# A down product copied from PSUM in one piece, its halves summed later from SBUF, and seven table values loaded per round on TensorE

## The chip, the core and the metric

The kernel runs on one core of a Trainium2 chip. The core has five engines with instruction queues of their own: TensorE (PE in the rows, its weight loads PEld), VectorE (DVE), ScalarE (ACT), GpSimd (POOL) and SyncE (SP), which here only issues transfers. They meet through semaphores. The metric is the device time of one launch in microseconds. Three runs of the kernel before took 306.15, 307.87 and 311.05 us.

## The reference

Two sequences of 1024 tokens of width 256 go through a layer norm and a cross attention to 77 context rows, then a layer norm and a feed-forward part with one shared expert and 32 routed ones, of which each token takes one:

```python
x = x + xattn(layernorm(x), ctx, ctx, mask, ...)
h = layernorm(x).reshape(-1, 256)
shared = (silu(h @ shared_gate) * (h @ shared_up)) @ shared_down     # 256 -> 512 -> 256
logits = h @ gate_w                                                  # 32 experts
e = argmax(logits); score = sigmoid(max(logits))
g, u = (h * score) @ routed_gate[e], (h * score) @ routed_up[e]      # 256 -> 512
routed = (silu(g) * u) @ routed_down[e]                              # 512 -> 256
x = x + shared + routed
```

All of it is in float32. An expert has 1.5 MB of weights: 0.5 MB each for gate, up and down.

## The kernel before, in words

Attention, norms and routing come first. The tokens are then sorted by expert with indirect transfers, and the shared expert's products fill TensorE in between. What matters here is the **expert loop** behind that.

The sorted tokens are cut into *chunks* of 32 tokens of one expert, at least one chunk for each expert: 79 with these inputs, in experts of 3, 3, 2, 2, 5, 1, 7, 2, 5, 1, 1, 3, ... chunks. A table in SBUF (chunk_cum, made on VectorE) holds where each expert's chunks end, counted from the first. TensorE's loop is a hardware loop over 5 *rounds* of 6 experts, and a rest of 2 experts. The weights lie in a ring of 6 slots (ring_gu, ring_d): SyncE refills a slot (refill, L355) with the expert 6 further on as soon as the last chunk of the expert in it has its gate and up products (u_done), then the down weights (down_done). SyncE takes the slots strictly in order.

A chunk goes through the engines thus:

- GpSimd copies the chunk's 32 columns of the transposed tokens to x_c, in two halves (L455, L457). For this it loads the chunk's first column from a table each time (L453).
- TensorE does the gate and up products (gate_up, L1016) into bank 0 and bank 1 of PSUM, 16 matmuls each that count as 32 passes in the profile. It may overwrite bank 0 when Silu has read it (silu_done) and bank 1 when the gated product has read it (h_ready).
- ScalarE does Silu of bank 0 (L775), VectorE multiplies by bank 1 (gated, L643) and transposes (turn_h, L647) into the single buffer hT, when the down product of the chunk before has read it (down_done).
- TensorE does the down product (down_of, L1038) into bank 2. The two halves of the inner sum lie on partitions 0 to 63 and 64 to 127, and have to be added.
- ScalarE copies the low half to SBUF (take_half, L780), VectorE adds the high half to it from PSUM (take_y, L653) and signals y_ready. The next down product waits for y_ready, since there is one bank for it.
- Every 16 chunks ScalarE issues two stores of finished rows (store_y, L783).

TensorE's order is skewed by one chunk: the gate and up products of a chunk stand ahead of the down product of the chunk before. Written out, expert() does an expert's first chunk (L1047 to L1054), in whose middle the sequencer loads turn_end, where the expert ends. The remaining chunks follow in an inner loop behind a branch (L1056 to L1059). At a round's start it also loads turn_first (L1064). Each value_load is a TENSOR_LOAD and two instructions that check the value's range (shown as ISA in lists of instructions, as FUSED_REGOPS and SEQ_ASSERT in the trace).

Behind the loop the last stores land, GpSimd gathers the rows back in token order (L462, 16 transfers), VectorE adds them to the residual and SyncE writes them out.

## Time and profile before

| | |
|---|---|
| Runs, us | 306.15, 307.87, 311.05; median 307.87 |
| The profiled execution, us | 305.98 |
| its span, first to last instruction, us | 304.2 |
| mean granted TensorE clock | 0.974 |
| TensorE matmuls busy | 261.5 us, 86% |
| VectorE, ScalarE, GpSimd busy | 51%, 31%, 29% |
| Moved by DMA | 68.69 MB, mean 226 GB/s |
| Gate, up and down products of the expert loop, busy | 86.5 us and 51.0 us |

Busy time is a share of the whole span. The span has stages with different limits, so the table does not say what a change in the expert loop is worth. That is read from the timeline of the loop, where each line gives the start, the length, the engine, the line of the kernel, what is written and read, and in brackets how long the engine had been idle and which instruction ended that. "issue" means that nothing the profile shows was waited for.

### The profile page before, as it was taken

The numbers are of one execution on the slowest core, as the hardware profiler recorded it, in microseconds if no ns is written. First come the engines' busy times: TensorE is split into PE (matmuls) and PEld (weight loads), VectorE is DVE, ScalarE is ACT, GpSimd is POOL, SyncE is SP. The second block draws the span as 40 slices with busy tenths as digits, with TensorE's granted clock in tenths as the row PEclk, the third lists the DMA queues.
The fourth block names the chain that finished last, engine by engine and source line by source line (L and its number), as shares of the span: only waits on it lengthen the run. The fifth ranks groups of instructions, "written<-read, shape, count | busy, mean of one in ns | idle before, by whom it ended". The sixth has DMA issues, their size and how long they took to land.

```text
span 304.2 us, 12929 instructions
## 1 busy us (share of the span) xinstructions
PE 261.5 (86%) x4628; PEld 183.6 (60%) x4629; DVE 155.4 (51%) x490; ACT 93.7 (31%) x284; POOL 88.0 (29%) x248
## 2 busy tenths in 40 slices
PE   4978999998798999979889999899899899889710
PEld 3736656653473488657667777677677677643600
DVE  0547877884599321145454555455455455423423
ACT  2056766542311102243232333233233233212000
POOL 1245121111017764022222222222222222202772
PEclk9996899999999999999999999999999999999995
DMA  6999994000002235209989599999999999524575
GB/s 197 343 371 374 375 372 147 0 3 2 0 0 95 103 99 188 69 4 321 321 291 312 155 317 301 367 386 385 371 375 382 384 371 373 186 48 110 165 207 163
DMA packets 53039, 68.69 MB, mean 226 GB/s; under 512 B 3966, under 2 KB 35099, under 8 KB 53019
## 3 DMA queue, kind: packets, MB, share of 16 engines
q1 hardware_dynamic: 46203, 61.60, 58.9%
q0 software_dynamic: 1536, 4.20, 4.5%
q10 hardware_dynamic: 5280, 2.62, 3.3%
q8 instruction: 13, 0.21, 0.3%
q14 instruction: 7, 0.06, 0.1%
HBM read 59.49 MB, written 8.91 MB: 225 GB/s over the span
## 4 chain that ended last, share of the span: by engine, by line
PE 70%; DVE 8%; issue 7%; POOL 5%; DMA 4%; ACT 4%; POOLq 1%; ACTq 1%; SPq 1%; DVEq 0%
PE bank L1016 26%; PE bank L1038 15%; PE bank L941 13%; PE bank L953 5%; POOL xs_flat L462 4%; PE bank L872 3%; PE bank L907 2%; DMA slot_rows<-late 2%; DVE h_place L530 1%; PE bank L890 1%; DVE h_place L531 1%; DMA bq_row<-in_L_xattn_bias_q_dram 1%; ACT h_place L740 1%; DMA xs_flat<-slot_rows,slot_i 1%; PE bank L845 1%
## 5 line engine op out<-in xcount | busy, mean ns | idle before, releaser
L1016 PE MATMUL bank<-ring_gu,x_c 128*32 128x128 f32 x2528 | 86.5, 275 | 7.9 <-issue 5.9
L1016 PEld LDWEIGHTS bank<-ring_gu,x_c 128*32 128x32 f32 x2528 | 65.9, 109 | 23.3 <-issue 20.5
L1038 PE MATMUL bank<-ring_d,h_place 128*32 128x128 f32 x1264 | 51.0, 276 | 4.4 <-DVE late L653 1.0
L455 POOL COPY x_c<-xs_flat 128x32 f32 x79 | 16.6, 210 | 99.1 <-PE bank L1016 86.6
L1038 PEld LDWEIGHTS bank<-ring_d,h_place 128*32 128x32 f32 x1264 | 32.2, 108 | 19.3 <-issue 17.1
L643 DVE TENSOR_TENSOR h_place<-h_place,bank 128x128 f32<-128x128 f32 x79 | 22.7, 288 | 40.2 <-ACT h_place L775 40.2
L780 ACT COPY late<-bank 64x128 f32 (+1 forms) x79 | 20.5, 259 | 51.9 <-PE bank L1038 51.9
L775 ACT ACTIVATE h_place<-bank 128x128 f32<-128x128 f32 x79 | 21.9, 278 | 44.0 <-PE bank L1016 44.0
L647 DVE STREAM_TRANSPOSE h_place<-h_place 128x128 f32<-128x128 f32 x79 | 24.6, 311 | 14.4 <-PE bank L1038 9.8
L953 PE MATMUL bank<-shd,h_place 128*128 128x256 f32 x128 | 28.4, 380 | 2.1 <-DVE h_place L531 2.1
L653 DVE TENSOR_TENSOR late<-bank,late 64x128 f32 x79 | 23.1, 293 | 13.8 <-ACT late L780 12.5
L953 PEld LDWEIGHTS bank<-shd,h_place 128*128 128x128 f32 x128 | 24.2, 190 | 6.7 <-DVE h_place L531 3.0
L530 DVE SCALAR_TENSOR_TENSOR h_place<-h_place,bank 128x512 f32<-128x512 f32 x16 | 11.0, 686 | 32.4 <-ACT h_place L740 32.4
L941 PE MATMUL bank<-late,shg 128*128 128x512 f32 x48 | 23.1, 603 | 4.4 <-DVE h_place L531 4.3
L740 ACT ACTIVATE h_place<-bank 128x512 f32<-128x512 f32 x16 | 9.6, 597 | 52.0 <-PE bank L941 52.0
L941 PE MATMUL bank<-late,shu 128*128 128x512 f32 x48 | 22.6, 592 | 0.0
L457 POOL COPY x_c<-xs_flat 128x32 f32 x79 | 16.6, 210 | 17.1 <-PE bank L1016 16.9
L462 POOL DMA_INDIRECT xs_flat<-slot_rows,slot_i x16 | 15.2, 951 | 17.0 <-DMA slot_rows<-late 12.4
L438 POOL DMA_INDIRECT sorted_rows<-xs_flat,pos x16 | 16.1, 1006 | 11.1 <-DVE pos L593 6.5
L941 PEld LDWEIGHTS bank<-late,shg 128*128 128x128 f32 x48 | 8.5, 190 | 13.0 <-issue 7.2
L941 PEld LDWEIGHTS bank<-late,shu 128*128 128x128 f32 x48 | 9.1, 190 | 11.5 <-issue 11.5
L872 PE MATMUL bank<-ident,xs_flat 128*128 128x128 f32 x64 | 10.8, 295 | 2.0 <-DVE xs_flat L514 0.7
(133 smaller groups left out, 255.7 us busy)
## 6 DMA issues: line engine op xcount, KB each, us to landing
ring_gu<-L_ffn_routed_gate_w_dram SPq DMA_DIRECT2D x32, 512.0 KB, 8.5
ring_gu<-n_L_ffn_routed_up_w_dram SPq DMA_DIRECT2D x32, 512.0 KB, 9.5
ring_d<-L_ffn_routed_down_w_dram SPq DMA_DIRECT2D x32, 512.0 KB, 9.9
slot_rows<-late ACTq DMA_DIRECT2D x10, 256.0 KB, 5.8
x<-in_x_dram SPq DMA_DIRECT2D x4, 512.0 KB, 6.8
slot_rows<-zeros SPq DMA_DIRECT2D x1, 2048.0 KB, 14.4
late<-sorted_rows SPq DMA_DIRECT2D x8, 256.0 KB, 3.3
out_dram<-x SPq DMA_DIRECT2D x8, 256.0 KB, 2.4
```

The source lines that it names most:

```text
L455: g_.tensor_copy(x_c[:, 0], xsT[:, 0, bass.ds(col, LW)]).then_inc(x0_part, 1)
L462: g_.indirect_dma_start(out=y_t[:, i, :], out_offset=None, in_=slot_rows, in_offset=bass.IndirectOffsetOnAxis(ap=slot_i[:, i:i + 1], axis= ...
L643: v.tensor_tensor(h_r, g_silu, bank[1][:, 0:P], ALU.mult).then_inc(h_ready, 1)
L647: v.transpose(hT, h_r).then_inc(hT_ready, 1)
L653: v.tensor_tensor(rows, bank[2][HR:P, 0:DH], rows, ALU.add).then_inc(y_ready, 1)
L775: a_.activation(g_silu, bank[0][:, 0:P], ACT.Silu).then_inc(silu_done, 1)
L780: a_.copy(y_all[:, bass.ds(c, 1)].rearrange("p c d -> p (c d)"), bank[2][0:HR, 0:DH]).then_inc(half_taken, 1)
L872: ins = te.transpose(dst[:, c:c + P], src[:, a + j, k * P:(k + 1) * P], ident[:])
L941: ins = te.matmul(dst[:], w[:, k, m * P:(m + 1) * P], xnT_of(g)[:, k], start=(k == 0), stop=(k == KD - 1))
L953: ins = te.matmul(bank[4 + w % 2][:, j * D:(j + 1) * D], h_s[:, w // 2 % 2, m, c:c + P], shd[:, m], start=(m == 0), stop=(m == KF - 1))
L1016: ins = te.matmul(bank[g][q * LW:(q + 1) * LW, 0:P].rearrange("p (m f) -> p m f", f=LW), x_c[:, k], columns[:, q], start=(k == 0), stop=(k ...
L1038: ins = te.matmul(bank[2][r:r + LW, 0:DH], hT[:, f * LW:(f + 1) * LW], ring_d[:, s, f, a * DH:(a + 1) * DH], start=(m == 0), stop=(m == HA ...
```

## The change

Four things change together.

1. take_y moves to ScalarE and copies the whole 128 partitions of the down product to SBUF in one instruction. It signals a new semaphore, y_taken, and the next down product waits for this instead of y_ready.
2. The sum of the two halves (sum_y) is done by VectorE with both operands in SBUF, one chunk later than before: in the loop behind the transpose of chunk c it sums chunk c-2. Two sums follow the loop. y_ready now counts sums alone, so the stores' waits lose their offset of 2.
3. The tables turn_first and turn_end become one table, turn, with 1 in front. At the start of a round TensorE loads seven neighbouring values of it at once (three for the rest), and none inside the round.
4. The round is rotated. The first gate and up products are done ahead of the loop; in a round each expert first does its remaining chunks (other_chunks), then the first gate and up products of the next expert followed by its own last down product (next_expert). The branch on the first round goes. The products come in the same order as before.

```diff
-        y_all = late[0:HR, 0:SLOTS * DH].rearrange("p (c d) -> p c d", c=SLOTS)
+        y_halves = late[:, 0:SLOTS * DH].rearrange("p (c d) -> p c d", c=SLOTS)
+        y_all = y_halves[0:HR]
...
-            v.tensor_scalar(turn_end[:], chunk_cum[0:1], 1.0, None, ALU.add).then_inc(table_ready, 1)
-            v.scalar_tensor_tensor(out=turn_first[:], in0=chunk_cum[0:1], scalar=1.0, in1=chunk_f[0:1],
-                                   op0=ALU.add, op1=ALU.subtract).then_inc(table_ready, 1)
+            v.memset(turn[:, 0:1], 1).then_inc(table_ready, 1)
+            v.tensor_scalar(turn[:, 1:NE + 1], chunk_cum[0:1], 1.0, None, ALU.add).then_inc(table_ready, 1)
...
-            def take_y(c):
-                dve.wait_ge(half_taken, c + 1)
-                rows = y_all[:, bass.ds(c, 1)].rearrange("p c d -> p (c d)")
-                v.tensor_tensor(rows, bank[2][HR:P, 0:DH], rows, ALU.add).then_inc(y_ready, 1)
+            def sum_y(c):
+                dve.wait_ge(y_taken, c + 1 + FREE2)
+                sums = y_all[:, bass.ds(c, 1)].rearrange("p c d -> p (c d)")
+                other = y_halves[HR:P, bass.ds(c, 1)].rearrange("p c d -> p (c d)")
+                v.tensor_tensor(sums, other, sums, ALU.add).then_inc(y_ready, 1)
...
-            with dve.Fori(1, n_chunks) as c:
+            gated(1)
+            dve.wait_ge(down_done, 1)
+            turn_h(1)
+            with dve.Fori(2, n_chunks) as c:
                 gated(c)
                 dve.wait_ge(down_done, c)
                 turn_h(c)
-                take_y(c - 1)
-            take_y(n_chunks - 1)
+                sum_y(c - 2)
+            sum_y(n_chunks - 2)
+            sum_y(n_chunks - 1)
...
-            def take_half(c):
+            def take_y(c):
                 act.wait_ge(down_done, c + 1)
-                a_.copy(y_all[:, bass.ds(c, 1)].rearrange("p c d -> p (c d)"), bank[2][0:HR, 0:DH]).then_inc(half_taken, 1)
+                a_.copy(y_halves[:, bass.ds(c, 1)].rearrange("p c d -> p (c d)"), bank[2][:, 0:DH]).then_inc(y_taken, 1)
...
-                        act.wait_ge(y_ready, STORE * b + FREE2)
+                        act.wait_ge(y_ready, STORE * b)
...
             def down_of(w, s):
                 pe.wait_ge(hT_ready, w)
-                pe.wait_ge(y_ready, w)
+                pe.wait_ge(y_taken, w)
...
-            def expert(w, e, s, before, landed):
-                pe.wait_ge(gu_in[s], 2 * landed)
-                gate_up(w, s)
-                end = pe.value_load(turn_end[0:1, bass.ds(e, 1)], min_val=2, max_val=MAX_CHUNKS + 1)
-                if before is None:
-                    with pe.If(it > 0):
-                        down_of(w, RING - 1)
-                else:
-                    down_of(w, before)
+            def turns(e, n):
+                _, values = nc.values_load_multi_w_load_instructions(
+                    turn[0:1, bass.ds(e, n)], engines=(mybir.EngineType.PE,), min_val=1, max_val=MAX_CHUNKS + 1)
+                return values
+            def other_chunks(w, end, s, landed):
                 pe.wait_ge(d_in[s], landed)
                 with pe.If(w + 1 < end):
                     with pe.Fori(w + 1, end) as more:
                         gate_up(more, s)
                         down_of(more, s)
                     pe.nop()
-                return end
+            def next_expert(end, s, landed):
+                n = (s + 1) % RING
+                pe.wait_ge(gu_in[n], 2 * landed)
+                gate_up(end, n)
+                down_of(end, s)
+            pe.wait_ge(gu_in[0], 32)
+            gate_up(1, 0)
             with pe.Fori(0, ROUNDS) as it:
-                w = pe.value_load(turn_first[0:1, bass.ds(RING * it, 1)], min_val=1, max_val=MAX_CHUNKS)
+                w = turns(RING * it, RING + 1)
                 for s in range(RING):
-                    w = expert(w, RING * it + s, s, s - 1 if s else None, 16 * it + 16)
+                    other_chunks(w[s], w[s + 1], s, 16 * it + 16)
+                    next_expert(w[s + 1], s, 16 * it + (16 if s + 1 < RING else 32))
...
```

The first place is the start of a round on TensorE's queue. Before, with the load of turn_first ahead of the gate and up products (L1016) and that of turn_end behind them, ahead of the down product (L1038):

```order
L1063 UNCONDITIONAL_BRANCH
L1063 ISA
L1064 TENSOR_LOAD turn_first
L1064 ISA x2
L1047 ISA
L1016 MATMUL bank<-ring_gu,x_c 32x128 [waits silu_done,x0_part,gu_in0]
...
L1016 MATMUL bank<-ring_gu,x_c 32x128 x7
L1049 REGISTER_ALU
L1049 TENSOR_LOAD turn_end
L1049 ISA x2
L1051 COMPARE_AND_BRANCH
L1038 MATMUL bank<-ring_d,h_place 32x128 [waits y_ready,hT_ready]
```

Now the same place, and what follows it up to the inner loop (gate and up products are L1020, down products L1042):

```order
L1020 MATMUL bank<-ring_gu,x_c 32x128 x7
L1072 UNCONDITIONAL_BRANCH
L1072 ISA
L1050 TENSOR_LOAD turn
L1050 ISA x14
L1056 ISA
L1057 REGISTER_ALU [waits d_in0]
L1057 COMPARE_AND_BRANCH
L1058 UNCONDITIONAL_BRANCH
L1020 MATMUL bank<-ring_gu,x_c 32x128 [waits silu_done,x0_part]
```

The seven loads of a round have become one, at its start, with fourteen instructions of checks behind it, and the checks of all seven values stand ahead of the first product that follows; between gate and down products nothing is left.

The second place is VectorE's loop over chunks. Before:

```order
L642 REGISTER_ALU [waits u_done,silu_done]
L643 TENSOR_TENSOR h_place<-h_place,bank 128x128 [waits hT_ready]
L647 STREAM_TRANSPOSE h_place<-h_place 128x128 [waits h_ready,down_done]
L653 ISA [waits half_taken]
L653 TENSOR_TENSOR late<-bank,late 64x128
```

Now:

```order
L641 REGISTER_ALU [waits u_done,silu_done]
L642 TENSOR_TENSOR h_place<-h_place,bank 128x128 [waits hT_ready]
L646 STREAM_TRANSPOSE h_place<-h_place 128x128 [waits h_ready,down_done]
L653 ISA [waits y_taken]
L653 REGISTER_ALU
L653 TENSOR_TENSOR late<-late 64x128
```

The sum stands where the add stood, but it is that of the chunk before, and its input from PSUM (bank) is gone.

## Rows read from the trace of the kernel before

**Rows 1.** The page: clock granted, DMA engines' share, GB/s, in 40 slices.

```profile
PEclk9996899999999999999999999999999999999995
DMA  6999994000002235209989599999999999524575
GB/s 197 343 371 374 375 372 147 0 3 2 0 0 95 103 99 188 69 4 321 321 291 312 155 317 301 367 386 385 371 375 382 384 371 373 186 48 110 165 207 163
```

**Rows 2.** Timeline, inner loop: start us, us, engine line op tiles count [idle before <-releaser].

```profile
164.32 0.65 PE L1038 MATMUL bank<-ring_d,h_place 128*32 128x128 f32 x16
...
165.04 0.31 DVE L647 STREAM_TRANSPOSE h_place<-h_place 128x128 f32<-128x128 f32 x1
165.11 0.26 ACT L780 COPY late<-bank 64x128 f32 x1 [0.58 <-PE bank L1038]
165.52 0.29 DVE L653 TENSOR_TENSOR late<-bank,late 64x128 f32 x1 [0.17 <-ACT late L780]
...
165.96 0.64 PE L1038 MATMUL bank<-ring_d,h_place 128*32 128x128 f32 x16
```

**Rows 3.** Timeline where TensorE comes sooner than its inputs.

```profile
171.26 0.21 POOL L457 COPY x_c<-xs_flat 128x32 f32 x1
...
171.32 1.18 PE L1016 MATMUL bank<-ring_gu,x_c 128*32 128x128 f32 x32
171.64 0.59 PEld L1016 LDWEIGHTS bank<-ring_gu,x_c 128*32 128x32 f32 x24 [0.16 <-DVE h_place L643]
...
172.32 0.21 POOL L455 COPY x_c<-xs_flat 128x32 f32 x1 [0.85 <-PE bank L1016]
172.35 0.28 ACT L775 ACTIVATE h_place<-bank 128x128 f32<-128x128 f32 x1 [0.44 <-PE bank L1016]
...
172.61 0.64 PE L1038 MATMUL bank<-ring_d,h_place 128*32 128x128 f32 x16
...
172.75 0.29 DVE L643 TENSOR_TENSOR h_place<-h_place,bank 128x128 f32<-128x128 f32 x1 [0.39 <-ACT h_place L775]
```

**Rows 4.** Timeline of TensorE: first product of rounds four and six.

```profile
216.72 1.08 PE L1016 MATMUL bank<-ring_gu,x_c 128*32 128x128 f32 x32 [1.02 <-issue]
...
262.03 1.08 PE L1016 MATMUL bank<-ring_gu,x_c 128*32 128x128 f32 x32 [0.82 <-issue]
```

**Rows 5.** Sequencer instructions between two rounds: ns min/median/max, first, last start us.

```profile
L1064 PEldq TENSOR_LOAD <-turn_first x1: 309/309/309, 241.7 to 241.7; - x1
L1064 PEldq FUSED_REGOPS  x1: 146/146/146, 242.1 to 242.1; - x1
...
L1047 PEldq FUSED_REGOPS  x1: 51/51/51, 242.4 to 242.4; - x1
```

**Rows 6.** Timeline of TensorE: chunk products that the sums count from.

```profile
132.93 1.09 PE L1016 MATMUL bank<-ring_gu,x_c 128*32 128x128 f32 x32 [1.60 <-ACT h_place L775]
133.84 0.62 PE L1038 MATMUL bank<-ring_d,h_place 128*32 128x128 f32 x16
...
148.66 0.85 PE L1016 MATMUL bank<-ring_gu,x_c 128*32 128x128 f32 x20 [0.67 <-issue]
...
181.44 1.08 PE L1016 MATMUL bank<-ring_gu,x_c 128*32 128x128 f32 x32
...
266.94 1.08 PE L1016 MATMUL bank<-ring_gu,x_c 128*32 128x128 f32 x32
...
269.74 0.65 PE L1038 MATMUL bank<-ring_d,h_place 128*32 128x128 f32 x16 [1.01 <-DVE late L653]
```

**Rows 7.** Weight transfers: two issues in the timeline, and us to landing.

```profile
182.73 0.38 SPq L311 DMA_DIRECT2D ring_gu<-L_ffn_routed_gate_w_dram  x1
...
253.80 1.16 SPq L315 DMA_DIRECT2D ring_d<-L_ffn_routed_down_w_dram  x1
...
ring_d<-L_ffn_routed_down_w_dram SPq DMA_DIRECT2D x1, 512.0 KB, 10.2
```

More of the change, by code:

```diff
@@ L188, in build_cross_attention_moe @@
         begin = sb("begin", [1, P], I32)
-        turn_first = sb("turn_first", [1, NE], I32)
-        turn_end = sb("turn_end", [1, NE], I32)
+        turn = sb("turn", [1, NE + 1], I32)
         block_n = sb("block_n", [1, 1], I32)
@@ L269, in build_cross_attention_moe @@
         begin_ready = sem("begin_ready")
-        half_taken = sem("half_taken")
+        y_taken = sem("y_taken")
         g_done = sem("g_done")
@@ L793, in _ @@
                 if j:
-                    take_half(j - 1)
+                    take_y(j - 1)
             with act.Fori(1, blocks) as b:
@@ L797, in _ @@
                     silu(STORE * b + j)
-                    take_half(STORE * b + j - 1)
+                    take_y(STORE * b + j - 1)
                     if j == 3:
-                        act.wait_ge(y_ready, STORE * b + FREE2)
+                        act.wait_ge(y_ready, STORE * b)
                     if j in (3, 8):
@@ L804, in _ @@
                 silu(c)
-                take_half(c - 1)
-            take_half(n_chunks - 1)
-            act.wait_ge(y_ready, STORE * blocks + FREE2)
+                take_y(c - 1)
+            take_y(n_chunks - 1)
+            act.wait_ge(y_ready, STORE * blocks)
             for a in range(HALVES):
                 store_y(blocks - 1, a)
-            act.wait_ge(y_ready, n_chunks + FREE2)
+            act.wait_ge(y_ready, n_chunks)
             for a in range(HALVES):
@@ L819, in _ @@
             te = nc.tensor
-            for credit in (y_ready, y_ready, silu_done, h_ready, hT_ready, x0_used, u_done):
+            for credit in (y_taken, y_taken, silu_done, h_ready, hT_ready, x0_used, u_done):
                 pe.sem_inc(credit, FREE1)
@@ L1060, in expert @@
                     pe.nop()
-                return end
+            def next_expert(end, s, landed):
[5 more added lines that the diff above has]
+            gate_up(1, 0)
             with pe.Fori(0, ROUNDS) as it:
-                w = pe.value_load(turn_first[0:1, bass.ds(RING * it, 1)], min_val=1, max_val=MAX_CHUNKS)
+                w = turns(RING * it, RING + 1)
                 for s in range(RING):
-                    w = expert(w, RING * it + s, s, s - 1 if s else None, 16 * it + 16)
-            w = pe.value_load(turn_first[0:1, RING * ROUNDS:RING * ROUNDS + 1], min_val=1, max_val=MAX_CHUNKS)
+                    other_chunks(w[s], w[s + 1], s, 16 * it + 16)
+                    next_expert(w[s + 1], s, 16 * it + (16 if s + 1 < RING else 32))
+            w = turns(RING * ROUNDS, REST + 1)
             for s in range(REST):
-                w = expert(w, RING * ROUNDS + s, s, s - 1 if s else RING - 1, 16 * ROUNDS + 16)
+                other_chunks(w[s], w[s + 1], s, 16 * ROUNDS + 16)
+                if s + 1 < REST:
+                    next_expert(w[s + 1], s, 16 * ROUNDS + 16)
             down_of(n_chunks + 1, REST - 1)
             shared_up(3 * KF + 1)
-            pe.wait_ge(y_ready, n_chunks + FREE2)
+            pe.wait_ge(y_taken, n_chunks + FREE2)
             shared_up(3 * KF + 2)
```

## The prediction

> **What bounds the kernel now.** I read the slices of the page first [rows 1]. The expert loop fills slices 18 to 36 (130.3 to 270.4 us), with the TensorE clock at full all through it. From slice 26 to 34 the DMA engines are 9 tenths busy at 367 to 386 GB/s, before that they have holes. So two things can set the pace: the loop of engines, and behind it, in its second half, the stream of expert weights.
>
> The timeline of the inner loop [rows 2] then shows which wait ends last. A down product starts at 164.32 and the next at 165.96: 1.64 us for a chunk. Between them ScalarE copies the low half (it starts 0.79 after the product), VectorE adds the high half (0.41 later, since the transpose that starts at 165.04 is ahead of it), the add takes 0.29, and 0.15 after its end the next product starts: 0.79 + 0.41 + 0.29 + 0.15 = 1.64. This cycle through one PSUM bank is closed by y_ready, and it sets the chunk.
>
> The next cycle is seen where TensorE happens to come early [rows 3]. The gate and up products start at 171.32 and stop after 8 weight loads, until the gated product of the chunk before is out of the banks (h_ready); they go on at 171.64. From there: Silu 0.71 later, the gated product 0.40 after that, 0.29 long, and, as at 171.64, some 0.05 to TensorE: 1.45 us. TensorE itself needs less: 0.91 from the gate products to the down product [rows 6], and some 0.4 for the down product, 1.3 in all.
>
> In the same rows the down product starts 1.29 after its gate products (171.32 to 172.61) rather than 0.91. This is the first chunk of an expert, where TensorE's sequencer loads turn_end between the two.
>
> **The change, part by part.**
>
> *One copy, the sum later.* The down product now waits for the copy alone: 0.79 + 0.26 + 0.15 = 1.20, and for the transpose: 0.72 + 0.31 + 0.15 = 1.18 [rows 2]. Both are under 1.45, so the cycle of rows 3 becomes the bound. The copy covers 128 partitions instead of 64; its cost is by the column, as the Silu of 128x128 at 0.28 beside the copy of 64x128 at 0.26 shows [rows 3, 2], so I add 0.02 at most, hidden. The add keeps its size and moves one chunk later; VectorE has 0.29 + 0.31 + 0.29 of work in 1.45, so it is hidden, unless it disturbs another engine (rivals). The last sum before the stores is the same in both kernels.
>
> *The table loads.* Before, 32 loads stand between gate and down products at some 0.3 us of delay each; they go, and with y_ready gone nothing but 1.45 holds these chunks either. The rotated round itself issues the same products in the same order. From the second chunk's gate products (132.93) to the last chunk's (266.94) [rows 6] there are 77 periods in 134.0 us, 1.74 each with everything. After: 77 x 1.45 = 111.7. The stall of 0.67 before 148.66 has no semaphore behind it; I keep it.
>
> *The round's start.* Before, TensorE idles 1.02 us between rounds and 0.82 at the last one [rows 4]: branch, one load, one check. The load takes 0.4 to its check (241.7 to 242.1), the check of one value 0.3 (242.1 to 242.4) [rows 5]. Seven values come in one load instruction but with seven pairs of checks. Nothing shows a seven-word load; I take it as one, and 0.28 for each further check. Between rounds that is 6 x 0.28 = 1.7, plus 0.3 for the wait and the branch of the inner loop that now stand there, less 0.2 that the sequencer has in hand when it no longer waits for y_ready: idle 2.8. The period there is 0.91 + 0.64 + 2.8 = 4.3 instead of 1.45, so 2.85 on top, four times: 11.4. At the last boundary three values: 0.82 + 2 x 0.28 + 0.3 - 0.2 = 1.5 idle, 1.6 + 1.4 - 1.45, about 1.4 on top. The bounds for one further check are its two instructions alone, 0.16, and a whole load with check, 0.7; 0.28 is nearest to the row.
>
> *The first round.* Its seven loads come behind the first gate products. The sequencer is done with those at about 130.5; branch, load, seven checks, wait and inner loop take 3.2, so the second chunk starts at 133.7 rather than 132.93: 0.8 lost.
>
> TensorE alone: 111.7 + 11.4 + 1.4 + 0.7 = 125.2 against 134.0, 8.8 saved, less 0.8: 8.0.
>
> *The stream.* The DMA engines are last not full around 182 to 184; then the gate weights issued at 182.73 start a stretch that is full up to the last down weights, issued at 253.80 and landed 10.2 later, at 264.0 [rows 7, 1]. The last chunk's gate products come at 266.94, 2.9 later. That slack is all there is: the stretch moves the same bytes at the same rate, so it ends earlier only by as much as it begins earlier. It begins when the 30th chunk's products (181.44) free their slot. Up to there are 28 periods, 48.5 us before; after, 28 x 1.45 + 2.85 + 0.7 = 44.2, so 4.3 less 0.8: 3.5 earlier. The last down weights land at 260.5, and with 0.3 of waits and branch the last gate products start at 260.8, 6.1 earlier, where TensorE alone would be 8.0 earlier. TensorE therefore waits some 2 us for weights near the end.
>
> *The end.* From the last gate products to the start of the last down product it takes 2.80 (266.94 to 269.74), after it 0.91 + 1.20 = 2.1: 0.7 more. From there to the end the chain runs through stores, GpSimd's gathers and the output, which the change leaves alone.
>
> **Sum:** 6.1 + 0.7 = 6.8, I take 6.9 with a tenth for the copy's earlier start. Against the profiled execution's 305.98 (span 304.2 and 1.8 around it) that is 299.1. The median of the runs is 307.87, 1.9 above the profiled one; at the same distance I expect 301.0.
>
> **The rivals.**
>
> 1. *The period falls only to 1.52 or more.* GpSimd needs 1.06 from its second copy to the next first one (171.26 to 172.32) [rows 3] and at least 0.2 to the next second: near 1.3. The new sum reads two SBUF operands, once per chunk, just when the copy of x_c is due. If one holds up the other by its 0.29, GpSimd needs 1.5 to 1.6. Then 77 x 0.07 = 5.4 or more of the 8.8 goes: 3.4 saved, 304.5; at 1.56 nearly nothing. For it speaks only the closeness; against it that the delay need not fall on the same path each time. The Trainium skill has this rule in "SBUF — State Buffer", section "SBUF: two separate sides": VectorE with two SBUF inputs and a GpSimd operation that reads SBUF exclude each other for the whole instruction. No row here has that pair side by side, so whether the trace agrees is open. Chance 0.15.
>
> 2. *The stream doesn't move.* If transfers are late for another reason than the slot release at 182.7, the last weights still land at 264.0 and 2.9 - 0.3 + 0.7 = 3.3 is all: 304.6. Chance 0.12.
>
> 3. *The stream gives way.* The part up to slice 25 runs below the later rate; with issues coming sooner it may catch up. Then TensorE alone counts, 8.0 + 0.7: 299.2, or 298 with cheaper checks. Chance 0.12.
>
> 4. *Slower: the clock falls between rounds.* TensorE stands for 2.8 us instead of 1.0, four times. The page shows the clock down in slices 4 and 5 [rows 1], some 7 us at half, and no fall at the gaps of 1.0 and 1.6 in the loop [rows 4, 6]. If each new gap costs 7 us at half clock, a chunk there needs 2 x 1.3 = 2.6, 2.7 chunks lose 1.15 each, 3.1 a time, 12.4 in all: 8.7 - 12.4, so 3.7 slower, 311.6. It decides from three falls on. Chance 0.06. The Trainium skill, "TensorE: Matmul & The Clock Gate", section "What's actually happening", says that activity releases the throttle and idleness brings it back; the rows agree in direction.
>
> 5. *Slower: a seven-word load costs as seven loads.* Six more at 0.4 on four rounds, two at the last, six at the first: 12.8 lost, 4.1 slower, 312.0. The single load instruction speaks against it. Chance 0.05.
>
> **How the numbers follow.** The forecast has 0.5, with 5 to 8 us saved (299.9 to 302.9), since the checks (0.16 to 0.35) move both the rounds and the release of the slot. A difference of 2 per cent, 6.2 us or below 301.7, is about what a measurement of this kernel tells from none. About two thirds of the forecast's case (0.33), rival 3 (0.12) and little else lie below: 0.47 faster. Rivals 1 and 2, the rest of the forecast and most of 4 and 5 (under 314.0) are within: 0.49. Slower by more: 0.04. The range from 297.8 to 306.5 takes in the forecast, rivals 2 and 3 and most of rival 1, and leaves out 4 and 5.
>
> **What would show it.** In the timeline: down products 1.45 apart in the inner loop, with weight loads of the gate products held by the gated product; 0.9 between gate and down products in an expert's first chunk; idle of 2.8 between rounds and 1.5 at the last, clock at full; and waits of TensorE for ring_gu or ring_d only in the last two experts. Periods above 1.5 with TensorE waiting for x_c would mean rival 1. The prediction is wrong above all if the gaps between rounds exceed 4 us, or if the last weights do not land near 260.5.

## The result: slower by 2.9 per cent, where a little faster was forecast

| | before | after |
|---|---|---|
| median of 4 runs each, us | 307.01 (306.07 to 311.05) | 315.46 (313.24 to 317.93) |
| the profiled execution, us | 305.98 | 313.24 |
| its span, us | 304.2 | 311.3 |
| mean granted clock | 0.974 | 0.941 |

The ratio is 1.029, 95% interval 1.018 to 1.040. So it is slower, though the runs do not settle whether by more than 2 per cent. The forecast was 301.0, range 297.8 to 306.5, with 0.04 on slower by more than 2 per cent. Here and below the medians are of all runs, while the ratios are taken to runs of the kernel before made beside them and compare the fast runs alone, since some executions of a kernel are slower without any change to it.

### The profile page after: what moved, and what is told of

It is laid out like the page before. It is cut to its first block, busy times and chain, and to the rows that moved or that the text cites. A ratio compares the mean times of both kernels' runs of the same rounds, so it can differ in the third digit from the quotient of the medians.

```text
span 311.3 us, 12946 instructions
## 1 busy us (share of the span) xinstructions
PE 258.1 (83%) x4627; PEld 192.1 (62%) x4629; DVE 154.6 (50%) x490; ACT 94.1 (30%) x284; POOL 87.8 (28%) x248
## 4 chain that ended last, share of the span: by engine, by line
PE 68%; issue 10%; DVE 8%; POOL 5%; DMA 3%; ACT 3%; POOLq 1%; ACTq 1%; SPq 0%; DVEq 0%
PE bank L1020 27%; PE bank L945 13%; PE bank L1042 12%; PE bank L957 4%; POOL xs_flat L462 4%; PE bank L876 3%; PE bank L911 2%; DMA slot_rows<-late 2%; DVE h_place L530 1%; PE bank L894 1%; DVE h_place L531 1%; ACT h_place L744 1%; DMA xs_flat<-slot_rows,slot_i 1%; DMA h_place<-in_L_xattn_kernel_q_dram 1%; PE bank L849 1%
## 5 line engine op out<-in xcount | busy, mean ns | idle before, releaser
L1020 PE MATMUL bank<-ring_gu,x_c 128*32 128x128 f32 x2528 | 97.3, 287 | 24.1 <-issue 23.7
L1020 PEld LDWEIGHTS bank<-ring_gu,x_c 128*32 128x32 f32 x2528 | 68.6, 114 | 41.9 <-issue 27.6
L1042 PE MATMUL bank<-ring_d,h_place 128*32 128x128 f32 x1264 | 53.0, 284 | 0.6 <-DVE h_place L646 0.6
L1042 PEld LDWEIGHTS bank<-ring_d,h_place 128*32 128x32 f32 x1264 | 39.3, 115 | 0.9 <-DVE h_place L646 0.8
L784 ACT COPY late<-bank 128x128 f32 (+1 forms) x79 | 21.0, 265 | 42.6 <-PE bank L1042 42.6
L957 PE MATMUL bank<-shd,h_place 128*128 128x256 f32 x128 | 30.1, 396 | 2.1 <-DVE h_place L531 2.1
L957 PEld LDWEIGHTS bank<-shd,h_place 128*128 128x128 f32 x128 | 25.3, 199 | 7.2 <-DVE h_place L531 3.0
L653 DVE TENSOR_TENSOR late<-late x79 | 22.4, 284 | 3.3 <-ACT late L784 0.8
```

The source lines that it names most:

```text
L653: v.tensor_tensor(sums, other, sums, ALU.add).then_inc(y_ready, 1)
L784: a_.copy(y_halves[:, bass.ds(c, 1)].rearrange("p c d -> p (c d)"), bank[2][:, 0:DH]).then_inc(y_taken, 1)
L957: ins = te.matmul(bank[4 + w % 2][:, j * D:(j + 1) * D], h_s[:, w // 2 % 2, m, c:c + P], shd[:, m], start=(m == 0), stop=(m == KF - 1))
L1020: ins = te.matmul(bank[g][q * LW:(q + 1) * LW, 0:P].rearrange("p (m f) -> p m f", f=LW), x_c[:, k], columns[:, q], start=(k == 0), stop=(k ...
L1042: ins = te.matmul(bank[2][r:r + LW, 0:DH], hT[:, f * LW:(f + 1) * LW], ring_d[:, s, f, a * DH:(a + 1) * DH], start=(m == 0), stop=(m == HA ...
```

## The profile after

The page of the changed kernel, in the view of [rows 1]:

```profile
PEclk9996999999999999979996999999979989999785
DMA  6999992000002354009978199999999999615564
GB/s 204 350 372 371 371 375 85 0 3 2 0 18 105 110 161 148 0 6 315 347 259 298 34 313 345 371 387 381 372 370 317 377 374 374 230 29 113 168 206 162
```

Slices are 7.8 us long. In the expert loop, slices 18 to 36, the clock dips four times (slices 18, 22, 30 and 33); in [rows 1] it does not.

The inner loop in the timeline, to be laid beside [rows 2, 3]:

```profile
210.62 0.62 PE L1042 MATMUL bank<-ring_d,h_place 128*32 128x128 f32 x16
210.65 0.28 ACT L779 ACTIVATE h_place<-bank 128x128 f32<-128x128 f32 x1 [0.45 <-PE bank L1020]
...
211.05 0.29 DVE L642 TENSOR_TENSOR h_place<-h_place,bank 128x128 f32<-128x128 f32 x1 [0.43 <-ACT h_place L779]
...
211.39 0.27 ACT L784 COPY late<-bank 128x128 f32 x1 [0.46 <-PE bank L1042]
211.39 0.59 PEld L1020 LDWEIGHTS bank<-ring_gu,x_c 128*32 128x32 f32 x24 [0.17 <-DVE h_place L642]
211.44 0.31 DVE L646 STREAM_TRANSPOSE h_place<-h_place 128x128 f32<-128x128 f32 x1
211.78 0.28 DVE L653 TENSOR_TENSOR late<-late  x1
...
212.07 0.62 PE L1042 MATMUL bank<-ring_d,h_place 128*32 128x128 f32 x16
212.09 0.21 POOL L455 COPY x_c<-xs_flat 128x32 f32 x1 [0.88 <-PE bank L1020]
```

Down products are 1.45 apart (1.64 in [rows 2]). The weight loads of the gate products stop until the gated product is out, as in [rows 3]: the cycle that the prediction named is now the bound. The copy of 128 partitions takes 0.27 (0.26 for 64 before), the sum from SBUF 0.28. The sum ends at 212.06, just ahead of GpSimd's copy, and neither is longer than before. The copy comes 0.70 after the weight loads go on (211.39 to 212.09), as in [rows 3], where no sum of two SBUF operands was near (171.64 to 172.32, 0.68).

The timeline of TensorE at the start of the loop, at a stall in the first round, at the second, third, fourth and fifth round, and at the end:

```profile
134.37 1.94 PE L1020 MATMUL bank<-ring_gu,x_c 128*32 128x128 f32 x32 [3.25 <-issue]
...
153.44 0.38 PE L1020 MATMUL bank<-ring_gu,x_c 128*32 128x128 f32 x2 [2.59 <-issue]
...
162.30 0.62 PE L1042 MATMUL bank<-ring_d,h_place 128*32 128x128 f32 x16
167.08 1.93 PE L1020 MATMUL bank<-ring_gu,x_c 128*32 128x128 f32 x32 [4.16 <-issue]
168.76 1.11 PE L1042 MATMUL bank<-ring_d,h_place 128*32 128x128 f32 x16
169.61 1.96 PE L1020 MATMUL bank<-ring_gu,x_c 128*32 128x128 f32 x32
...
200.90 1.08 PE L1020 MATMUL bank<-ring_gu,x_c 128*32 128x128 f32 x32 [3.50 <-issue]
201.77 0.65 PE L1042 MATMUL bank<-ring_d,h_place 128*32 128x128 f32 x16
202.24 1.18 PE L1020 MATMUL bank<-ring_gu,x_c 128*32 128x128 f32 x32
...
225.56 1.08 PE L1020 MATMUL bank<-ring_gu,x_c 128*32 128x128 f32 x32 [4.10 <-issue]
226.43 1.04 PE L1042 MATMUL bank<-ring_d,h_place 128*32 128x128 f32 x16
227.17 2.01 PE L1020 MATMUL bank<-ring_gu,x_c 128*32 128x128 f32 x32
...
252.85 1.08 PE L1020 MATMUL bank<-ring_gu,x_c 128*32 128x128 f32 x32 [3.46 <-issue]
253.72 1.02 PE L1042 MATMUL bank<-ring_d,h_place 128*32 128x128 f32 x16
254.44 2.01 PE L1020 MATMUL bank<-ring_gu,x_c 128*32 128x128 f32 x32
...
274.72 1.18 PE L1020 MATMUL bank<-ring_gu,x_c 128*32 128x128 f32 x32
...
276.91 0.81 PE L1042 MATMUL bank<-ring_d,h_place 128*32 128x128 f32 x16 [0.57 <-DVE h_place L646]
```

The second to fifth rounds begin behind idle of 4.16, 3.50, 4.10 and 3.46, the last behind 1.67. Before, the second began behind 1.38, the next three behind 1.02 and the last behind 0.82 (two of these in [rows 4]). Behind the gap at 167.08 the gate and up products take 1.93 instead of 1.08, and the next chunk begins 2.53 later, not 1.45: TensorE runs at 1.2 GHz. The table by stage (stretch, its length, busy time and count, granted clock, DMA share, GB/s) shows it as a clock of 0.63 in a stretch behind a gap, beside one between gaps:

```profile
172.00:197.00 25.00, 24.63 (x816) 1.00 0.75 251
225.50:229.60 4.10, 4.04 (x95) 0.63 1.06 371
```

Lastly the sequencer's instructions of the round loads (ns min/median/max, first and last start):

```profile
L1050 PEldq FUSED_REGOPS  x38: 146/146/151, 131.7 to 271.1; - x38
L1050 PEldq SEQ_ASSERT  x38: 18/18/18, 131.9 to 271.3; - x38
L1050 PEldq TENSOR_LOAD <-turn x6: 775/1084/1717, 130.6 to 269.7; - x6
```

The checks are what they were. The load of seven words takes 1.08 or 1.72, against 0.309 for one word in [rows 5]: 1.09, 1.72, 1.08, 1.71 and 1.08 at rounds one to five, and 0.78 for the three words of the last.

## The experiments

**Theory A** from here on: the period is 1.45 as forecast and worth its gain; the loss comes from the round's start alone, where the load is three to six times as long as taken, and where the longer idle lets the clock fall. The rivals differ by experiment.

### Each half of the change alone

The first kernel takes the one copy and the later sum, with the expert loop of before. The second takes the rotated loop and leaves the down product's way as it was.

```diff
 # copy alone: bank 2 out in one copy, the sum a chunk later; loop as before
-  a_.copy(y_all..., bank[2][0:HR, 0:DH]).then_inc(half_taken, 1)
+  a_.copy(y_halves..., bank[2][:, 0:DH]).then_inc(y_taken, 1)
-  pe.wait_ge(y_ready, w)
+  pe.wait_ge(y_taken, w)
 # loads alone: the rotated loop with turns(), y_ready as before
-  w = expert(w, RING * it + s, s, ...)
+  other_chunks(w[s], w[s + 1], s, ...); next_expert(w[s + 1], s, ...)
```

> The whole-height copy on ScalarE with the sum one chunk later, but TensorE's expert loop and its table loads as before. Theory A (the copy is a gain, the loads cost): down products inside an expert 1.45 us apart, an expert's first chunk still 1.8, idle between rounds 1.0 and the clock at full through the loop; 46 chunks gain 0.1 to 0.15 each, so 4 to 6 us faster than before, near 302. Theory B (the sum from two SBUF operands or TensorE's denser work costs): GpSimd's copies of x_c or the clock suffer here too, and it is as slow as the change, near 315.

> The rotated round with its seven loads at once, but the down product copied and added as before. Theory A: idle of 3.4 to 4.2 us between rounds, the clock at half behind most of them, and chunks 1.64 apart: slower than before by 12 to 18 us, near 322, and slower than the whole change. Theory B: no slower than before, 307 or less, since the loads leave the experts' first chunks.

Measured: copy alone 303.40 (ratio 0.986, interval 0.982 to 0.991); loads alone 327.99 (1.067, 1.055 to 1.079). The copy gains and the loads lose, as Theory A says, though the loads cost more than its 12 to 18 us. They cost 20.4 us on top of before and 12.1 on top of the copy, and the periods from gate products to gate products say why. In the third round of the loads-alone kernel the first chunk of each further expert takes 1.76 to 1.82, as in before (1.77 to 1.81), since y_ready holds it anyway: the loads moved there give nothing back. With the copy alone these chunks take 1.84 to 1.99 (a few, behind an expert of one chunk, 1.71 to 1.74), in the change 1.45: some 22 x 0.42 is 9 us, which the gaps then cost and more.

These first chunks are one reason why the copy alone gains 4 us and not the 8.0 that I forecast for TensorE alone. The other is smaller, some 1.2 us, and is in its timeline of TensorE, near the end:

```profile
256.35 1.08 PE L1022 MATMUL bank<-ring_gu,x_c 128*32 128x128 f32 x32 [0.79 <-DMA ring_gu<-n_L_ffn_routed_up_w_dram]
...
260.46 1.08 PE L1022 MATMUL bank<-ring_gu,x_c 128*32 128x128 f32 x32 [0.69 <-DMA ring_gu<-n_L_ffn_routed_up_w_dram]
...
262.33 1.08 PE L1022 MATMUL bank<-ring_gu,x_c 128*32 128x128 f32 x32 [0.21 <-issue]
```

TensorE waits for weights twice there, as forecast for a faster loop. The last down weights land at 261.7, and the last gate products start 0.6 later.

### Fewer checks in the gap, and the clock held up

One kernel loads the seven values as the change does, but checks only two of them ahead of the round and each other one between an expert's gate and down products. The other leaves the checks and puts four products of 512 columns, which nothing reads, ahead of each round's load.

```diff
 # checks spread
-  turn[...], engines=(PE,), min_val=1, max_val=MAX_CHUNKS + 1)
+  turn[...], engines=(PE,), min_val=None, max_val=None)
+  w[0], w[1] = checked(w[0]), checked(w[1])      # ahead of the round
+  w[s + 2] = checked(w[s + 2])                   # behind gate_up of expert s + 1
 # filled gap
   with pe.Fori(0, ROUNDS) as it:
+      for _ in range(4):
+          te.matmul(bank[3][:], shg[:, 0, 0:P], xnT_last[:, 0], start=True, stop=True)
       w = turns(RING * it, RING + 1)
```

> The whole change, but the seven values are loaded without their range checks; two are checked at the round's start, each other one between the gate and down products an expert ahead of its use. Theory A with the checks as the larger part of the idle time: idle between rounds falls by 1.4 us, to 2.1, or 2.7 where the load is a long one, the clock falls less often, and the time comes to 300 to 307. If the load itself is what costs, idle falls by under 0.5 and the time stays over 312.

> The whole change, with four more 128x512 float32 matmuls into an unused bank ahead of the loads of each round of the loop, 3.4 us of array work that nobody reads, in the place of idle time. If the clock's fall behind the gaps is a real part of the loss, the clock stays at full in the loop and it is 5 to 7 us faster than the change, near 309. If the clock is only a sign, the time stays at 315 or rises by what the matmuls stick out of the gap.

Measured: checks spread 304.53 (0.993, 0.988 to 0.998), as expected; filled gap 307.57 (1.001, 0.996 to 1.007), a little faster than expected. The filled gap, in the timeline of TensorE at the second round:

```profile
161.84 3.70 PE L1074 MATMUL bank<-xnT_last,shg 128*128 128x512 f32 x8
166.43 1.08 PE L1020 MATMUL bank<-ring_gu,x_c 128*32 128x128 f32 x32 [0.90 <-issue]
167.30 0.65 PE L1042 MATMUL bank<-ring_d,h_place 128*32 128x128 f32 x16
167.78 1.18 PE L1020 MATMUL bank<-ring_gu,x_c 128*32 128x128 f32 x32
```

TensorE does 3.70 us more work here, the chunk behind the round starts 0.34 later than in the change (6.05 from gate products to gate products, not 5.71), and the kernel is 8 us faster. No stretch of its expert loop is at half clock. That is the clock's part, told apart from the gap's length: the stretches from round to round are no shorter (by the four periods 0.7 longer in all), and most of the loss is gone. In the profiles the loop from second to last chunk is 8.2 shorter (132.15 and 140.35). Of that 6.2 are the half-clock chunks, counted below, which the fillers removed. Another 0.9 is a shorter stall near 150 us and 0.8 one near 147 that is not there; nothing shows that the fillers did that, so I put 6 of the 8 us down to the clock.

With spread checks the gaps are 2.00 to 2.68, and the clock still falls behind three of four, as behind this one:

```profile
193.17 1.91 PE L1020 MATMUL bank<-ring_gu,x_c 128*32 128x128 f32 x32 [2.04 <-issue]
```

### The load by itself

The loads of 1.72 all started at words 6 and 18 of the table, those of 1.08 at words 0, 12 and 24. The next kernel gives each round a row of eight words; another loads all eight of them (four at the last round). Both have spread checks.

```diff
-  turn = sb("turn", [1, NE + 1], I32)
+  turn = sb("turn", [1, 8 * (ROUNDS + 1)], I32)
...
-  w = turns(RING * it, RING + 1)
+  w = turns(8 * it, RING + 1)          # aligned rows
+  w = turns(8 * it, 8)[:RING + 1]      # eight words
```

> As the kernel with one load and spread checks, but each round's seven values begin a row of eight words of the table, so every load starts at a multiple of 32 bytes; before they started at 0, 24, 48, 72, 96 and 120 bytes. Theory A (the seven-word load takes 1.08 or 1.71 by where its words begin: 1.71 at 24 and 72 bytes, 1.08 at 0, 48 and 96): all five loads at 1.08, gaps of the second and fourth round shorter by 0.63 each, median 1.3 us less than 304.5, near 303.2, or 302 if the clock then falls once less. Rival (the time is another thing of those rounds, such as the state of the sequencer's cache or traffic at that moment): loads at 1.71 in the same two rounds and 304.5 again.

> As the kernel with aligned rows and spread checks, but each round loads all eight words of its row (the eighth is not used) and the last one four. Theory A (a load's time goes by the pieces of a power of two that it is cut into: one word took 0.31, three (2+1) 0.78, seven (4+2+1) 1.08 where aligned and 1.71 at 24 and 72 bytes): eight words are at most two pieces of four, so 0.6 to 0.8 instead of 1.08, four at the last round 0.3 to 0.6 instead of 0.78; gap periods 0.3 to 0.4 shorter, at most 1.2 us in all, of which the weight stream (loop end 265 to 268 in all spread kernels) leaves little: median 302.5 to 304.5. Rival (the time goes by words, some 0.13 each): eight words take 1.2, four 0.75, gap periods 0.1 longer, median 304 to 305.

Measured: aligned rows 304.00 (0.987, 0.982 to 0.992), all five loads 1.07 to 1.10; eight words 301.71 (0.981, 0.971 to 0.990), with these loads:

```profile
L1056 PEldq TENSOR_LOAD <-turn x6: 346/594/617, 130.6 to 258.1; - x6
```

Eight words take 0.59 to 0.62, seven take 1.08. So a load's time goes by where its words begin, as expected, and not by their number alone; the kernel with eight words came out below its range, by 0.8 us. Its round gaps are 1.52 to 1.59, and behind none of these four does the clock fall. The third round:

```profile
191.15 1.12 PE L1026 MATMUL bank<-ring_gu,x_c 128*32 128x128 f32 x32 [1.52 <-issue]
192.02 0.69 PE L1048 MATMUL bank<-ring_d,h_place 128*32 128x128 f32 x16
192.51 1.18 PE L1026 MATMUL bank<-ring_gu,x_c 128*32 128x128 f32 x32
```

To learn what a load's time goes by, the changed kernel got 17 more loads ahead of the loop. In a first version nothing used the values:

> The changed kernel with 17 further table loads on TensorE's sequencer ahead of the expert loop, whose values nothing uses: 1 to 8 words from byte 0, 7 words from word 1, 2, 3, 4 and 6, 2 and 4 words from word 1, 4 from word 2 and 4. It is run for the durations of these loads. Theory A (pieces of a power of two): 1, 2, 4 words alike near 0.3 to 0.5, 3, 5 and 6 near 0.8, 7 near 1.1, 8 under 1.1; 7 words from word 4 as from 0 (1.1), from words 2 and 6 1.7, from words 1 and 3 1.7 or longer. Rival (by words): 0.3 plus 0.13 for each further word wherever they start. The loads take some 12 to 18 us, of which the wait for the first weights and values hides a part: time 318 to 332.

The loads were dropped when it was built, so this says nothing of them. It is a second look at the changed kernel: 316.78, gap periods of 5.69, 5.08, 5.72 and 5.06, and this time half clock behind all four. In the second version the last value of each load is checked:

```diff
+  for at, n in ((0, 1), (0, 2), ..., (0, 8), (1, 7), (2, 7), (3, 7), (4, 7), (6, 7), (1, 2), (1, 4), (2, 4), (4, 4)):
+      _, some = nc.values_load_multi_w_load_instructions(turn[0:1, at:at + n], engines=(PE,), ...)
+      nc.s_assert_within(some[n - 1], 1, MAX_CHUNKS + 1)
```

> The changed kernel with 17 further table loads on TensorE's sequencer ahead of the expert loop; the last value of each is checked, so that the load is kept: 1 to 8 words from word 0, 7 words from word 1, 2, 3, 4 and 6, 2 and 4 words from word 1, 4 from word 2 and 4. Run for the durations of these loads. Theory A (pieces of a power of two, which start at a multiple of their own size): 1, 2 and 4 words 0.31 to 0.4, 8 words 0.6, 3, 5 and 6 near 0.6 to 0.8, 7 near 1.08; 7 words from word 4 as from 0, from word 2 and 6 at 1.71, from words 1 and 3 at 1.1 to 1.7; 4 words from word 1 over 0.6. Rival (by words): falsified already by 8 words at 0.60; another rule by start alone would make all loads from words 1, 2, 3 and 6 longer by the same 0.6. The loads take some 13 to 18 us ahead of the loop, partly beside the shared products: 320 to 332.

Its time, 336.89, is of no interest. The sequencer's loads, window by window, in the order of the diff: 1, 4, 7 and 8 words from word 0, then 7 from word 1, 4 from word 1, 4 from word 4:

```profile
L1074 PEldq TENSOR_LOAD <-turn x1: 323/323/323, 132.1 to 132.1; - x1
L1074 PEldq TENSOR_LOAD <-turn x1: 344/344/344, 134.8 to 134.8; - x1
L1074 PEldq TENSOR_LOAD <-turn x1: 1062/1062/1062, 137.6 to 137.6; - x1
L1074 PEldq TENSOR_LOAD <-turn x1: 595/595/595, 139.0 to 139.0; - x1
L1074 PEldq TENSOR_LOAD <-turn x1: 1711/1711/1711, 139.9 to 139.9; - x1
L1074 PEldq TENSOR_LOAD <-turn x1: 997/997/997, 150.6 to 150.6; - x1
L1074 PEldq TENSOR_LOAD <-turn x1: 341/341/341, 153.3 to 153.3; - x1
```

| words, from word 0 | 1 | 2 | 3 | 4 | 5 | 6 | 7 | 8 |
|---|---|---|---|---|---|---|---|---|
| ns | 323 | 557 | 767 | 344 | 611 | 830 | 1062 | 595 |

Seven words take 1711, 1708, 1701 and 1697 from words 1, 2, 3 and 6, and 1064 from word 4. Two from word 1 take 534, four from word 2 take 997.

So the pieces are not the powers of two that I expected (two words should then have taken 0.31 to 0.4). They are words one by one, at some 0.23 each, and groups of four at 0.25, the latter only where the load starts at a multiple of four words. Seven from word 0 are one group and three words, 0.1 + 4 x 0.24; from word 6 they are seven words, 0.1 + 7 x 0.23. All the loads above fit that within 0.04; that a load that starts off such a multiple uses no group later on either is shown by 7 words from word 1.

### The change with a cheap load, and nothing else

```diff
-  w = turns(RING * it, RING + 1)        # seven words, seven checks
+  w = turns(8 * it, 8)[:RING + 1]       # eight words from an aligned row
+  w = [checked(v) for v in w]           # seven checks, all ahead of the round
```

> The changed kernel as it is, all seven checks ahead of the round, but with aligned rows and a load of eight words (four at the last round). What failed in the prediction was the load: taken as 0.31, measured 1.08 and 1.71. Theory A (the load's excess made the gap 3.5 to 4.2 instead of 2.8): loads at 0.60, gaps 2.9 to 3.1 at all four rounds, 1.3 at the last, that is 0.5 + 1.1 + 0.5 + 1.1 + 0.4 = 3.6 us less of idle, and the half clock behind the gaps stays in part: median 309 to 312.5. If the clock stays at full behind gaps of 3.0: 305 to 308. Rival (the load is not what the gap waits for, or the clock's fall takes all of it): 314 to 316 again.

Measured 309.12 (1.003, 0.997 to 1.008), where the change has a ratio of 1.029: some 8 us less. In the profiles the loop from second to last chunk is 6.4 shorter, 3.7 of it in the round gaps, as expected; the rest is in the stalls of the first round, in the half-clock chunks and in single waits. In the timeline of TensorE at the fourth round:

```profile
217.17 0.62 PE L1048 MATMUL bank<-ring_d,h_place 128*32 128x128 f32 x16
220.78 1.93 PE L1026 MATMUL bank<-ring_gu,x_c 128*32 128x128 f32 x32 [2.99 <-issue]
222.46 1.07 PE L1048 MATMUL bank<-ring_d,h_place 128*32 128x128 f32 x16
223.31 1.09 PE L1026 MATMUL bank<-ring_gu,x_c 128*32 128x128 f32 x32
```

The gaps are 3.05, 2.98, 2.99 and 3.01: with a load of 0.60 what the prediction's sum gives (2.8 with a load of 0.31). The last is 1.20, 0.3 less than its sum. The clock falls behind three of the four even so. This kernel has about the gaps that I forecast, and it is not faster than before. So a short load alone would not have made the forecast come true. The clock's fall, which I gave 0.06, stands against it, and with it the stall near 150 us, 2.1 of idle in this kernel.

### What else could be had

Two fillers instead of four, with spread checks, and the same with aligned rows; and the copy alone with each check moved behind the down product.

```diff
 # two fillers
+  for _ in range(2):
+      te.matmul(bank[3][:], shg[:, 0, 0:P], xnT_last[:, 0], start=True, stop=True)
   w = turns(...)
 # check behind the down product
-  end = pe.value_load(turn_end[...], min_val=2, max_val=MAX_CHUNKS + 1)
+  end = loaded(turn_end, bass.ds(e, 1))                  # no check here
   down_of(w, ...)
+  end = nc.s_assert_within(end, 2, MAX_CHUNKS + 1)
```

> As the kernel with one load and spread checks, with two filler products of 512 columns ahead of each round's load, which nothing reads. Theory A (four stretches at half clock of 3.4 us behind the gaps cost the spread kernel some 0.9 to 1.6 us each): no half clock in the expert loop; the fillers themselves are 1.7 us of TensorE per round, of which the load behind them (1.08 to 1.71, on the sequencer) is no cover, since the load comes after they are issued but runs beside them: gap periods as in the spread kernel, +-0.4; loop end 267.1 - 4 = 263 to 265, median 300 to 302.5. Rival (the clock costs nothing there, the chunks are bound by ScalarE and VectorE also at half clock): 304.5 plus what the fillers add, 304.5 to 307.

> Both of the last two edits together: rows of eight words and two fillers ahead of each round's load. Theory A (load time by where the words begin, and the clock kept up, add): 0.5 to 1.3 us below the kernel with fillers alone, 299 to 301.5, unless the weight stream already ends the loop (last weights landed 263.7 in the spread kernel, 261.8 with the copy alone), in which case TensorE waits for ring_gu in the last two experts and it is the same as fillers alone. Rival (both hidden): 304.5 as the spread kernel.

> One copy and the later sum, with the one-word table loads of the kernel before, but the check of each value moved from between gate and down products to behind the down product. Theory A (what remains over 1.45 at an expert's first chunk is sequencer work of load and check, and the stream ends the loop): with the copy alone an expert's first chunk had some 0.15 to 0.3 of check on the path, so 32 x 0.15 = 3 to 5 us less on TensorE, of which the last weights (they landed at 261.8 with the copy alone) let through 1 or 2: median 300 to 302.5, loop end 263 to 265, and waits for ring_gu in the last two experts as with the copy alone or longer; no stretch at half clock in the loop. Rival (the first chunk is held by the load itself, or the check only moves its 0.28 to the branch behind the down product): no change from the copy alone, 303.4, loop end 265.3.

Measured: 302.94 (0.988, 0.983 to 0.992), 302.96 (0.983, 0.978 to 0.988) and 301.74 (0.986, 0.978 to 0.995). The first is 0.4 over its range, and the second is no better than the first, as was expected should the weight stream end the loop. Behind no round gap of the first two does the clock fall; in the first it falls once, behind the stall near 150 us. The third is the copy alone again, as its rival said: in the profiles of both an expert's first chunk takes 1.87 from gate products to gate products (207.17 to 209.04 with the copy alone, 209.50 to 211.37 here); the check only moved.

None of their medians is below 301.7, and the timeline of the second, near the end, shows what stands in the way:

```profile
258.39 1.08 PE L1024 MATMUL bank<-ring_gu,x_c 128*32 128x128 f32 x32 [2.65 <-DMA ring_gu<-n_L_ffn_routed_up_w_dram]
```

| | last down weights landed, us | last gate products | apart |
|---|---|---|---|
| before | 264.0 | 266.94 | 2.9 |
| after | 270.3 | 274.72 | 4.4 |
| filled gap | 266.5 | 268.77 | 2.3 |
| cheap load only | 266.2 | 268.31 | 2.2 |
| copy alone | 261.7 | 262.33 | 0.6 |
| checks spread | 263.6 | 264.19 | 0.5 |
| two fillers | 265.3 | 265.88 | 0.6 |
| eight words, spread | 262.2 | 262.70 | 0.5 |

(The landings are read from the semaphore events of the weight transfers.) In the last four kernels the loop ends with the weight stream. The eight-word kernel and the copy alone beat both kernels of this case, by 1 to 3 per cent against before; which of them is the better the runs do not tell, as their intervals overlap and they were not timed side by side.

## Why the prediction was wrong, point by point

From the second chunk's gate products to the last chunk's I forecast 125.2 us for TensorE alone; it took 140.35 (134.37 to 274.72). Each term, by the periods from gate products to gate products less 1.45:

| | forecast | measured |
|---|---|---|
| 77 periods of 1.45 | 111.7 | 111.7 |
| four round gaps and the last | 12.8 | 17.6 |
| chunks at half clock in the loop | 0 | 6.2 |
| stall near 150 us | 0.7 | 3.0 |
| other waits (0.8 of it a stall at 146.90) | 0 | 1.8 |

- *One copy, the sum later*: right. Period 1.45, by the cycle named. Rival 1 did not happen. By the rule of "SBUF — State Buffer" in the Trainium skill, section "SBUF: two separate sides", the sum and a GpSimd operation that reads SBUF exclude each other. Here the one ends just as the other begins, so the trace neither confirms the rule nor contradicts it; GpSimd's copy starts as long behind the weight loads as it did without such a sum (0.70 and 0.68).
- *The round's start*: **one of the two steps that failed.** "Nothing shows a seven-word load; I take it as one" was wrong by 0.77 or 1.41 a load. Between full rounds the rest of that sum was right: 2.8 plus 0.77 is 3.57 (3.50 and 3.46 measured), 2.8 plus 1.41 is 4.21 (4.16 and 4.10). Checks at 0.28 were right. At the last boundary the recorded sum has a slip (1.6 + 1.4 - 1.45 is 1.55, not 1.4); it measured 1.84, with a load of 0.78. I bounded the cost of a check from both sides and took the load at its lower bound. The upper one, rival 5, I put aside with the single instruction as the only reason; at rounds two and four the load comes near it (1.72 against 7 x 0.31 = 2.2).
- *The first round*: the second chunk starts at 134.37 instead of 133.7, the load again.
- *The clock*, rival 4: **the other step that failed, and the larger one.** The forecast's sum had nothing for it. It fell behind three of the four gaps and at the start, 6.2 us (forecast 12.4 if at all), against 5.5 that the loads cost in the gaps and at the start. The filled gap gave these 6.2 us back with the long loads in place, and the cheap load left three of the four falls in place. I gave it 0.06 because no gap of 1.0 to 1.6 in the loop had made it fall; a gap of 2.8 was outside what those rows could show. Counted by the idle ahead of it, the clock fell behind none of four gaps of 1.5 to 1.6 (eight words, spread), behind one of four of 2.0 to 2.1 (aligned rows), three of four of 2.0 to 2.7 (checks spread), three of four of 3.0 (cheap load), three of four of 3.5 to 4.2 and, in the second look, all four, and three of four of 3.7 to 4.4 (loads alone). It also fell behind the stall near 150 us in four kernels (idle of 1.9 to 3.2), and not behind it in others (1.7 to 2.8). The Trainium skill's "TensorE: Matmul & The Clock Gate", section "What's actually happening", has idleness bring the throttle back; the trace agrees, and it spoke against this change.
- *The stream*: the cap at the end is there, but this kernel came too late for it; the faster ones ran into it. Rivals 2 and 3 are out: the last weights moved with the loop, later here (264.0 to 270.3) and earlier with the copy alone (261.7), and they did not run ahead of it.
- *The stall* near 150 us without a semaphore I kept at 0.67. In the kernels with the rotated loop it is 1.7 to 3.2 of idle, 2.59 here. It comes in every one of them at the eleventh chunk, the first of the first round's fifth expert; here and with two fillers a shorter one (0.57 and 0.37) stands two chunks ahead of it. So 2.3 and 0.8 us of the miss are these stalls. No run was made to tell what they are; that stays open.
- *The end*: right, 2.19 to the last down product (2.1 forecast).

Together: 4.8 + 6.2 + 2.3 + 1.8 is 15.1 more in the loop, 0.7 more at its start, less 1.9 of waiting for the stream that did not come about: 13.9. The profiled time was 6.9 us less by forecast and 7.3 more by measurement, 14.1 apart. By cause, 6.2 are the clock, 5.5 mostly the loads (4.8 in the gaps, 0.7 at the start), 3.1 the stalls and 1.0 single waits, less the 1.9.

## What to carry to other kernels

Work moved off many short waits into one long one isn't only summed: ask of the one gap how long TensorE stands still, and price it at half clock behind it, above all where the rows show no gap of that length. A form of instruction that the trace doesn't show (a load of seven words instead of one) gets its own bounds, with the multiple of the known one as the upper; if it turns out dear, look at its size and start before giving it up. And read early what waits right behind the bound: here the weight stream ended 2.9 us ahead of the loop's last gate products, and it stood in the way of every faster version at about 302.

## What the runs showed of the hardware that I had not expected

- The sequencer's load of values takes 0.32 for one word and some 0.24 for each further piece, where a piece is four words if the load starts at a multiple of four words, and one word otherwise. Eight words (0.60) cost about what two (0.56) or five (0.61) do, and less than three (0.77) or seven (1.06).
- Products that nothing reads made the kernel 8 us faster than the change (307.57 and 315.46). They kept the clock at 2.4 GHz through a round's start, which is 6.2 of the 8.2 us that the loop is shorter in the profiles.
- Behind idle of equal length the clock sometimes falls and sometimes doesn't: behind 3.50 it stayed and behind 3.46 it fell in the same execution. It also fell behind 2.04 (checks spread) and 2.06 (aligned rows), and behind none of the four gaps of 1.52 to 1.59 (eight words).
